# An eight-slot in-place ring for the second-layer weights, a new order of stage one, and an unrolled main phase

## The reference

```python
node = x @ W1                                     # 4096 x 16
x0   = einsum('nk,nkf->nf', node, einsum('nc,kcf->nkf', x, W2))
x1   = layernorm(x + relu(adj @ x0 + node @ b))   # adj is 4096 x 4096
msg  = x1 @ W + B
wts  = where(adj < 1, exp(-(1/adj - 1)**2 / 0.5), 0)
out  = layernorm(x1 + wts @ msg)
```

## Time and profile before

| | before |
|---|---|
| runs | 615.05, 616.05, 617.22 us (median 616.05) |
| profiled execution | 615.5 us, its span 613.6 us |
| TensorE busy | 586.6 us (96%) |
| VectorE busy | 472.9 us (77%) |
| ScalarE busy | 457.6 us (75%) |
| GpSimd busy | 97.6 us (16%) |
| read from HBM | 139.81 MB |

### The profile page before, as it was taken

The page is one execution under the profiler, slowest core; times in us unless marked ns, Lnnn a source line. Parts: engine busy times, 40 slices in busy tenths (PEclk is TensorE's granted clock), DMA queues, the critical chain, the costliest instruction groups (busy, mean ns, idle before and its releaser), DMA issues.

```text
span 613.6 us, 5662 instructions
## 1 busy us (share of the span) xinstructions
PE 586.6 (96%) x1618; PEld 297.9 (49%) x1618; DVE 472.9 (77%) x541; ACT 457.6 (75%) x500; POOL 97.6 (16%) x75
## 2 busy tenths in 40 slices
PE   5999999998999999999999999999999999997886
PEld 4877777543444444444444444444444444443332
DVE  5999999807277787777777777777777777789994
ACT  2877668934377788778877778787877777889964
POOL 2678788700000000000000000000000000000320
PEclk9999999999999999999999999999999999998999
DMA  7920000387887787777767886787778777345302
GB/s 235 422 103 19 17 0 1 120 294 253 320 316 275 273 327 317 271 283 289 296 272 284 322 321 258 292 314 273 291 278 305 268 289 314 137 141 194 144 34 103
DMA packets 24480, 142.11 MB, mean 232 GB/s; under 512 B 2672, under 2 KB 4880, under 8 KB 8080
## 3 DMA queue, kind: packets, MB, share of 16 engines
q1 hardware_dynamic: 24464, 141.92, 60.0%
HBM read 139.81 MB, written 2.10 MB: 231 GB/s over the span
## 4 chain that ended last, share of the span: by engine, by line
PE 79%; DVE 9%; ACT 6%; issue 4%; DMA 1%; SPq 0%; DVEq 0%; ACTq 0%
PE acc_ps L329 35%; PE l_ps L363 31%; PE hw_ps L309 3%; DVE part_acc L579 3%; PE hw_ps L310 3%; PE hw_ps L311 3%; DVE wts L596 2%; ACT wts L465 2%; ACT wts L470 2%; DVE wts L606 1%; PE acc_ps L338 1%; PE msg_ps L352 1%; ACT wts L476 1%; DMA x_in<-xT_dram 1%; DVE x L583 1%
## 5 line engine op out<-in xcount | busy, mean ns | idle before, releaser
L363 PE MATMUL l_ps<-wts,msg 128*128 128x512 f32 x512 | 232.0, 597 | 6.5 <-DVE msg L630 4.0
L329 PE MATMUL acc_ps<-row_in,x 128*128 128x512 f32 x512 | 229.0, 592 | 0.0
L465 ACT ACTIVATE wts<-col_in 128x2048 f32<-128x2048 f32 x64 | 122.1, 1908 | 87.2 <-PE l_ps L363 75.2
L606 DVE SCALAR_TENSOR_TENSOR wts<-wts 128x2048 f32<-128x2048 f32 x64 | 147.4, 2304 | 40.6 <-ACT wts L470 40.6
L363 PEld LDWEIGHTS l_ps<-wts,msg 128*128 128x128 f32 x512 | 97.4, 191 | 131.4 <-issue 127.2
L329 PEld LDWEIGHTS acc_ps<-row_in,x 128*128 128x128 f32 x512 | 96.7, 190 | 118.7 <-issue 118.6
L596 DVE SCALAR_TENSOR_TENSOR wts<-col_in,wts 128x2048 f32<-128x2048 f32 x64 | 146.8, 2293 | 0.0
L470 ACT ACTIVATE wts<-wts 128x2048 f32<-128x2048 f32 x64 | 122.2, 1909 | 1.8
L476 ACT ACTIVATE wts<-wts 128x2048 f32<-128x2048 f32 x64 | 121.2, 1894 | 0.4 <-DVE wts L606 0.4
L764 POOL TENSOR_TENSOR row_in<-sumT 128x512 f32<-128x512 f32 x5 | 10.3, 2063 | 469.2 <-DVE sumT L706 469.2
L640 DVE TENSOR_TENSOR sumT<-l_ps,sumT 128x512 f32<-128x512 f32 x64 | 44.1, 690 | 52.9 <-PE l_ps L363 52.9
(11 more groups left out here) (52 smaller groups left out, 196.1 us busy)
## 6 DMA issues: line engine op xcount, KB each, us to landing
row_in<-adjT_dram SPq DMA_DIRECT2D x64, 1024.0 KB, 4.8
col_in<-adjT_dram SPq DMA_DIRECT2D x64, 1024.0 KB, 6.7
x_in<-xT_dram SPq DMA_DIRECT2D x8, 256.0 KB, 3.2
x_row<-xT_dram SPq DMA_DIRECT2D x8, 256.0 KB, 6.4
outT_dram<-sumT SPq DMA_DIRECT2D x8, 256.0 KB, 2.0
W_in<-W_dram SPq DMA_DIRECT2D x2, 512.0 KB, 4.5
B_sb<-B_dram SPq DMA_DIRECT2D x1, 256.0 KB, 4.3
W_sb<-W_dram SPq DMA_DIRECT2D x1, 64.0 KB, 3.7
```

Source lines behind the costliest of these rows:

```text
L329: mm = pe.matmul(acc_ps[:, :], x0[:, k, :], row_in[:, g % RING, c, :], start=(g == 0 and c == 0), stop=False)
L363: mm = pe.matmul(l1_ps[:, j % L1_BANKS, :], msg[:, k, :], wts[:, slot, k, :], start=(k == 0), stop=(k == CH - 1))
L465: act.activation(wts[:, slot, :, :], col_in[:, slot, :, :], ACT.Ln, bias=TINY).then_inc(ln_made, 1)
L606: dve.scalar_tensor_tensor(out=w, in0=w, scalar=2.0, in1=w, op0=ALU.subtract, op1=ALU.mult).then_inc(square_made, 1)
```

## The change

- `row_in` keeps four slots. `col_in` and `wts` become one ring `wt` of eight slots. A tile is loaded into a slot, masked there (`adj` where `adj < 1`, otherwise 0), turned into its logarithm, inverse, square and exponential in the same slot, and multiplied from it. The mask is now the first pass and the exponential the last. Slots 6 and 7 share their place with stage one's buffers, so they are first loaded when all sums and folds of stage one are done.
- The column tiles run twelve steps behind the row tiles (`COL_LAG`). Tiles 0 to 5 are made in every second step, one at a time; from tile 6 on one is made in every step.
- `sum_over_k` alternates between two groups of 128 nodes and keeps one sum for each; its last product writes `x0`, and the closing addition is gone. `round_x` and `node_product` of the next block stand in the middle of a block.
- The first loads: x, then three quarters of W2 on SyncE's queue; W1 and the first quarter of W2 on ScalarE's queue. Four row tiles and six column tiles are loaded during stage one.
- TensorE centres with a matrix (`centre_w`) in place of VectorE's subtraction, in both norms. GpSimd no longer squares in the tail. `acc_ps` has two banks; `W1b`'s product lies in a bank of stage one and waits for all its sums and products.
- No loops are left.

`SPLIT` is empty and `DVE_SQUARED` holds all eight columns, so the branches for split tiles and for ScalarE's square are never taken.

```diff
-        wts = sb("wts", [P, RING, CH, BW])
+        wt = [sb(f"wt_{s}", [P, CH, BW]) for s in range(WT_RING - LATE_SLOTS)]
+    def mask_step(m):
+        return exp_step(m) - 1
+    def exp_step(m):
+        return 2 * m + 1 if m < 6 else m + COL_LAG - 5
...
@@ sync
+            def load_wt(t):
+                at_least(sp, col_tile_done, t - WT_RING + 1)
+                sp.dma_start(wt[t % WT_RING][:, :, :], adjT[t % NB, t // NB]).then_inc(wt_in[t % WT_RING], 16)
...
+            for g in (2, 3):
+                load_x(g)
+            for i in range(ROW_RING):
+                load_row_tile(i)
+            for t in range(WT_RING - LATE_SLOTS):
+                load_wt(t)
+            for g in range(4, NB):
+                load_x(g)
+            sp.wait_ge(sum_step, NB * STEPS)
+            sp.wait_ge(fold_step, NB * FOLDS)
+            for t in range(WT_RING - LATE_SLOTS, WT_RING):
+                load_wt(t)
+            for i in range(TILES + COL_LAG):
+                if i % NB == 1 and i // NB + 1 < NB:
+                    load_x_row(i // NB + 1)
+                if i + ROW_RING < TILES:
+                    load_row_tile(i + ROW_RING)
+                t = i - COL_LAG
+                if t >= 0 and t + WT_RING < TILES:
+                    load_wt(t + WT_RING)
@@ tensor
+            pe.wait_ge(sum_step, NB * STEPS)
+            pe.wait_ge(prods_made, NB * GROUPS)
+            pe.matmul(w1b_ps, W1T_sb[:, :], b0_sb[:, :], start=True, stop=True).then_inc(w1b_made, 1)
...
+            for i in range(STEP_COUNT + 2):
+                r, g = i // NB, i % NB
+                if i < TILES:
+                    row_tile(i)
+                    if g == NB - 1:
+                        node_bias(r)
+                if g == 0 and 1 <= r <= NB:
+                    centre(r - 1)
+                if g == 3 and 1 <= r <= NB:
+                    messages(r - 1)
+                t = i - COL_LAG
+                if 0 <= t < TILES:
+                    col_tile(t)
+                if g == 1 and 1 <= r <= NB:
+                    variance(r - 1)
+                j = t - (TILES - NB)
+                if 0 <= j - 1 < NB:
+                    centre2(j - 1)
+                if 0 <= j - 2 < NB:
+                    variance2(j - 2)
@@ scalar
+            for i in range(STEP_COUNT + 2):
+                r, g = i // NB, i % NB
+                if g == 1 and 1 <= r <= NB:
+                    square(r - 1)
+                if g == 2 and 1 <= r <= NB:
+                    inverse_root(r - 1)
+                for t in exps_at.get(i, []):
+                    take_ln(t)
+                    take_inverse(t)
+                for t in left:
+                    take_exp(t)
...
@@ vector
-                    if q == QUARTERS - 1:
-                        dve.wait_ge(sum_step, g * STEPS + c * (K + 1) + K)
-                        dve.tensor_tensor(x0[:, bass.ds(g * CH + c, 1), :], part_acc[:, c, 0:1, :], part_acc[:, c, 1:2, :],
-                                          ALU.add).then_inc(sum_step, 1)
+                                out = x0[:, g * CH + c, :] if k == K - 1 else acc
+                    if q == 1 and g + 1 < NB:
+                        round_x(g + 1)
...
+            dve.wait_ge(fold_step, NB * FOLDS)
...
+            for i in range(STEP_COUNT + 4):
+                r, g = i // NB, i % NB
+                if g == 0 and 1 <= r <= NB:
+                    residual(r - 1)
+                if g == 4 and 1 <= r <= NB:
+                    copy_messages(r - 1)
+                if 0 <= i - COL_LAG - 1 < TILES:
+                    add_part(i - COL_LAG - 1)
...
+                for t in masks_at.get(i, []):
+                    mask(t)
+                if g == 2 and 1 <= r <= NB:
+                    scale_row(r - 1)
+                    add_row(r - 1)
+                for t in exps_at.get(i, []):
+                    if on_dve(t):
+                        take_square(t)
+                j = i - COL_LAG - (TILES - NB) - 3
+                if 0 <= j < NB:
+                    finish(j)
```

More of the change, by code:

```diff
@@ L239, in _ @@
-            load_x(0, 1)
+                sp.dma_start(x_in[:, g % 2, :], block_of(xT, g)).then_inc(x_in_sem[g % 2], 16)
+            load_x(0)
+            for q in range(1, QUARTERS):
+                load_W2(sp, q)
+            load_x(1)
             sp.dma_start(W1T_sb[:, :], W1T).then_inc(const_in, 16)
@@ L312, in hidden @@
                                   stop=True).then_inc(hw_made[half], 1)
[L314 to L330 removed]
+                    if n == GROUPS // 2 - 1 and g + 1 < NB:
+                        node_product(g + 1)
@@ L362, in col_tile, with centre2 @@
                 for k in range(CH):
-                    mm = pe.matmul(l1_ps[:, j % L1_BANKS, :], msg[:, k, :], wts[:, slot, k, :],
+                    mm = pe.matmul(l1_ps[:, t % L1_BANKS, :], msg[:, c % 2, k, :], wt[t % WT_RING][:, k, :],
                                    start=(k == 0), stop=(k == CH - 1))
                 mm.then_inc(col_tile_done, 1)
-            def row(r):
-                before = not isinstance(r, int) or r > 0
-                for g in range(NB):
-                    if before and not is_row(r, 1) and g == message_step(r):
-                        messages(r - 1)
-                    row_tile(r, g)
-                    if is_row(r, 1) and g == message_step(r):
-                        messages(r - 1)
+            def centre2(j):
+                pe.wait_ge(sum_added, TILES - NB + j + 1)
+                at_least(pe, out_made, j - 1)
+                pe.matmul(acc_ps[:, j % 2, :], centre_w[:, :], block_of(sumT, j), start=True,
+                          stop=True).then_inc(yc2_made, 1)
@@ new lines, in variance2 @@
+            def variance2(j):
+                pe.wait_ge(sq2_made, j + 1)
+                at_least(pe, ln_var2_made, j - 1)
+                pe.matmul(var2_ps[j % 2][:, :], mean_w[:, :], sq[:, j % 2, :], start=True,
+                          stop=True).then_inc(var2_made, 1)
+            pe.wait_ge(w1_in, 16)
+            node_product(0)
+            for g in range(NB):
+                hidden(g)
+            pe.wait_ge(const_in, CONSTS)
+            pe.wait_ge(sum_step, NB * STEPS)
+            pe.wait_ge(prods_made, NB * GROUPS)
@@ L410, in _ @@
-            pe.wait_ge(w1_in, 16)
-            node_product(0, 0)
-            for s in range(2):
-                first_stage(0, s)
-            with pe.Fori(1, NB // 2 - 1) as pair:
-                for s in range(2):
-                    first_stage(pair, s)
-            for s in range(2):
-                first_stage(NB // 2 - 1, s)
-            pe.wait_ge(const_in, CONSTS)
-            pe.wait_ge(node_copied, NB)
-            pe.matmul(w1b_ps, W1T_sb[:, :], b0_sb[:, :], start=True, stop=True).then_inc(w1b_made, 1)
@@ L424, in _ @@
-            pe.wait_ge(mean_w_filled, 1)
-            for r in (0, 1):
-                row(r)
-            with pe.Fori(2, NB - 1) as r:
-                row(r)
-            row(NB - 1)
-            for g in range(NB + TAIL_LAG + SCALE_LAG):
-                tail(g)
+                if g == 0 and 1 <= r <= NB:
[5 more added lines that the diff above has]
+                    col_tile(t)
@@ L542, in _, with take_ln @@
-            for r in (0, 1):
-                row(r)
-            with act.Fori(2, NB - 1) as r:
-                row(r)
-            row(NB - 1)
-            for g in range(NB + TAIL_LAG + SCALE_LAG):
-                tail(g)
+                    if n == GROUPS - 3 and g + 1 < NB:
+                        copy_node(g + 1)
+            def take_ln(t):
+                w = wt[t % WT_RING]
+                act.wait_ge(mask_made, t + 1)
+                act.activation(w[:, :, :], w[:, :, :], ACT.Ln, bias=TINY).then_inc(ln_made, 1)
@@ L663, in _ @@
+            round_x(0)
+            for q in range(QUARTERS):
+                split_W2(q)
+            for g in range(NB):
+                sum_over_k(g)
+                if g - 1 in SPLIT:
+                    split_x0(g - 1)
             for half in range(2):
                 dve.wait_ge(hw_made[half], NB * GROUPS)
+            dve.wait_ge(fold_step, NB * FOLDS)
+            for i in range(SPLIT_LEAD):
+                if is_split(i):
+                    split_row_tile(i)
+            if NB - 1 in SPLIT:
+                split_x0(NB - 1)
```

659 lines of the change are left out of this document (276 added, 383 removed).

## The result

The change made the kernel slower: 628.87 us median (626.45 to 630.18) against 616.23 (615.05 to 617.22) for the kernel before, a ratio of 1.020 [1.016, 1.024]. The prediction was 613.9 with a range of 606.5 to 621.5: the sign was wrong, and the time lies outside the range. The profiled execution took 630.18, its span is 628.4.

A forecast was written before the change was run, and what follows sets the result against it. VectorE bounds stage one, TensorE the main phase. Start -4.0, stage one -4.2, its end +2.25, ramp +5.9 and tail -2.1 sum to -2.15 us: 613.35 profiled, 613.9 median against 616.05, range 606.5 to 621.5.

The forecast's parts named there:

- The step that failed: Stage one: VectorE needs 10.6 us a block, under TensorE's 11.8; mid-block rounding of 2.1 makes TensorE wait 0.3 seven times.
- The seven node products: Stage one: 7 node products in TensorE's stream, counted as 6.0 us of the 97.2 us sum.
- E: End of stage one's last matmul, forecast at 103.6 us.
- Rival 1: Stage one stays VectorE's: x_lo always takes 2.78 us with GpSimd at work, 7.3 us more, 621.2, slower; 15%.
- Start: First loads: W1 starts at 0.75 on its own, so the first group starts at 6.4 instead of 10.39 us: -4.0.
- W1b's wait: End of stage one: W1b's product waits for VectorE's last 8 products, 2.3 us, delaying row tiles: +2.25.
- Ramp: Before the first column tile: four mask-to-square chains of 8.43 us delay row 0's centring; TensorE idles 6.8, low clock 1.8: +5.9.
- Tail: From step 64: messages wait 1.5, their copy 4.4, low clock 1.8, last norm 3.3; 11.0 lost, before 13.1: -2.1 us.
- Steady part and unrolling: Main phase: same TensorE work, loads in time, no gaps where looped rows end, so unrolling gives 0.

## Why the prediction was wrong, point by point

- **The step that failed** is "VectorE without the closing additions has 8.5 + 2.1 = 10.6 a block ... rounds for 2.1 ... a wait of 0.3 seven times". In the new place the rounding takes 4.14 us, nearly all of the excess being the cast's wait for a fold (2.50 where the sum has 0.45), and TensorE loses 13.57 - 11.8 = 1.8 a block, seven times. The duration of 0.45 for the cast was read from a place where another instruction had just waited in its stead; 1.64 for x_lo was about right (1.67). The price of a long rounding was set too high in turn: the forecast has 2.1 us cost 0.3, while the runs have 2.4 cost nothing, 2.77 cost 0.3 and 4.14 cost 1.8. (The seven node products are 7 x 0.81 = 5.7 us, where the sum has 6.0.) That E was 103.8 with the rounding in a better phase, against 103.6, is therefore two errors that cancel, start and waits.
- **Rival 1** named GpSimd as the cause and the block as the place, but put it on x_lo, the instruction with two inputs in SBUF, and left the cast at 0.45. Its price of 1.3 a block for a rounding of 3.2 was too high: between 0.3 at 2.77 and 1.8 at 4.14, some 0.8 (an estimate, on a line through these two). Its 621.2 was still nearer to the result than the forecast. Of its two signs, TensorE idle in each block came and x_lo at 2.5 or more did not.
- **Start**: -4.0 forecast, -1.7 measured. The first quarter of W2 was used at 7.41, too late for a first group at 6.4; five transfers of 256 KB had been asked for between 0.73 and 2.70. The other runs with these loads start at 7.35 to 8.50, so the gain was set some 1 us too high even for the best of them. Then 12 matmul passes followed each other 0.43 us apart (from 8.71 to 13.97), at half the normal pace, where the forecast had 8; that is 0.8 us of stage one's error. The forecast calls this the low clock; the granted clock in the profile reads 1.00 there.
- **W1b's wait**: +2.25 forecast, +1.7 measured.
- **Ramp**: +5.9 forecast, +7.6 measured. Mechanism, place and order right: four rounds of 8.41 (forecast 8.43), the centring waits 5.34 (6.8). Two low-clock stretches came in: 1.8 us in the 64 passes behind the wait for W1b's product (granted clock 0.63 from 119.35 to 124.00), which then shortened the centring's wait by as much, and 3.0 behind that wait, where 1.8 was forecast. No wait for a row tile shows in this trace; with the moved rounding two small ones do, hidden by the centring's wait as the forecast had it.
- **Tail**: -2.1 forecast, +0.3 measured. The gap is there (3.98, forecast 4.4), the messages wait 1.57 (1.5), the 16 slow passes lose 9.59 - 6.87 = 2.7 (1.8), and the last norm waits 2.17 + 1.83 = 4.0 (3.3). The rest is small: from the start of one instruction to that of the next, each of these four gaps is some 0.16 longer than the idle time that the profile gives, and the last pass has to run out.
- **Steady part and unrolling**: 0 forecast. TensorE has 50.00 of 50 us in both kernels; that taking the loops out saves nothing on it is as the earlier trace rows had shown. The Trainium skill's remark that kernels prefer full unrolling because a taken branch can stall the fetch (Runtime: NRT & Kernel Launch, Instruction fetch mechanics) gave nothing to be seen on TensorE here.

Errors: +2.3 at the start, +11.3 in stage one, -0.6, +1.7 and +2.4, the end -0.1: 17 us in spans. Stage one is two thirds of it, and all but about 1 us of that comes from one duration.

## What to carry to other kernels

When an instruction that waits for a shared resource is removed, look who comes next in its queue and needs the same resource: it can inherit the wait, so a duration read right behind a waiting instruction isn't that of the new place. In an in-order queue, the place of a step against another engine's regular rhythm can be worth more than its work: try neighbouring places before taking instructions out. And two chains that alternate mask and square run at the length of the whole chain; let the first half of the next tile go ahead of the second half of this one.
